# A two-layer graph network: one tile in four of layer 0's sums in fp32, layer 1's clearing and splits made ahead of its gathers, W1 and V2 loaded in four pieces

## The chip, the cores and the metric

One core of one Trainium2 chip runs the whole program. The metric is the device time of one execution in microseconds (us). Engines: TensorE (PE; its weight loads are PEld), VectorE (DVE), ScalarE (ACT), GpSimd (POOL), and SyncE (SP), which here only issues DMAs.

## The reference

1250 nodes with 512 features, 21250 edges sorted by their target `dst`. Layer 0 sums, for each node, messages built from the gathered source row and 64 edge features, and puts the sum through a two-layer MLP; layer 1 does the like with 128 edge features and a GRU update.

```
msg  = relu(x[src] + edge_attr_64 @ W_e + b_e)
h    = (1 + eps) * x + segment_sum(msg, dst)
h    = silu(bn(h @ W1 + b1)); h = silu(bn(h @ W2 + b2)); x = layernorm(x + h)

m    = relu(concat(x[src], edge_attr_128) @ V1.T + b1) @ V2.T + b2
agg  = segment_sum(m, dst)
gi, gh = agg @ W_ih.T + b_ih, x @ W_hh.T + b_hh      # gates r, z, n
out  = layernorm(x + x + bn((1 - z) * n + z * x))
```

All in fp32. Layer 1's `h[src] @ V1h` is computed once for each node into a table, and the edges gather rows of it. V2 is applied after the sum, b2 with the number of edges of each node.

## The kernel before, in words

Every engine runs a list of its own, in the order written, and they meet at semaphores. The edges are cut into 167 tiles of 128 (`TILES`); 4 tiles are a chunk (edge features and one-hot matrices are handled by chunks), 2 tiles a step, 12 tiles a window (`GROUP`), whose targets lie within 128 nodes.

Products of fp32 values are made from fp32r operands, each value split into a high part (the fp32r rounding) and a low part (the rest). For one tile of layer L:

- GpSimd gathers its 128 rows with one indirect DMA (line 429, `gather`) into a ring of 14 slots (`RAW`). The gather of tile t waits until the slot of tile t - 14 is read: for an odd tile `placed`, for an even one `low` (lines 425 to 428).
- SP loads the edge features by chunk into a ring of 3 (`load_chunk`, line 324). ScalarE makes the high part (`high_features`), VectorE the low one (`low_features`, line 1003).
- TensorE multiplies the features with W_e or V1e (`edge_product`, line 527): 2 products a tile in layer 0, 3 in layer 1. For an odd tile ScalarE first copies the gathered row into the bank (`place`, line 827 through `copy`), and the product adds to it; for an even one VectorE adds bank and row (`add_product`, line 1088).
- ScalarE makes `msg_hi`, the relu rounded to fp32r (`message_high`, line 866); VectorE makes `msg_lo`, relu minus `msg_hi` (`low_message`, line 1080). TensorE sums the tile by target: `hot` (one-hot, line 1074 on VectorE) times `msg_hi` and times `msg_lo` (`sum_product`, lines 551 and 552). In layer 1 it also counts the edges (`degrees`, line 565).
- After a window ScalarE copies the sum out of its bank (`sums`), TensorE turns it (`turn_window`, line 574), and VectorE adds it to `agg` at the window's first node (`add_window`, line 1103; the degrees at 1109).

`edges(L)` on each engine is the loop over the steps, with the sum two steps behind the product. Between the two comes layer 0's MLP (line 500, `product`), then the turn back to rows, the first layernorm and the table (`table_dram`), up to about 405 us; behind layer 1's edges come V2, the gates and the output.

What the change touches. In layer 1's gather loop GpSimd, after tile 13's gather, waits and clears `agg[1]` (four memsets, line 471) and `deg_r` (line 472). VectorE, after the last `table_sb`, splits half of the gate weights (`Wh_raw`, lines 1313 to 1315), V1e and v_b2 (to 1323), and then begins `edges(1)`; TensorE waits for V1e's split before `edges(1)` (line 728). SP loads W1 in one DMA behind chunk 9 of layer 0 (line 352), and V2 in one DMA as soon as the table is written (line 379), ahead of chunks 3 and later of layer 1.

## Time and profile before

| | us |
|---|---|
| median of 3 runs | 864.12 (863.08 to 864.97) |
| the profiled execution | 862.61 |
| its span, first to last instruction | 860.8 |
| PE / DVE / ACT / POOL busy | 787.4 / 656.0 / 449.8 / 350.7 |
| gathers of layer 0 start | 3.3 to 222.1 |
| first product of the MLP | 244.7 |
| gathers of layer 1 start | 408.4 to 626.4 |

Times of rows are counted from the span's start. A busy time covers an instruction from its start until its result is out; instructions of one engine overlap, so the distance between two starts can be smaller than the duration of one. In the timeline the brackets at the end of a row say how long the engine was idle before the instruction and what ended that.

### The profile page before, as it was taken

To read this page: it belongs to the slowest core of one execution; us is meant where nothing else is said; L and a number is where in the kernel's file an instruction comes from. 1 tells how busy PE (TensorE), PEld (TensorE's weight loads), DVE (VectorE), ACT (ScalarE), POOL (GpSimd) and SP (SyncE) were. 2 spreads that over 40 slices of the span, in tenths; PEclk is the share of its full clock that TensorE was granted. 3 is DMA by queue.
4 is the path that set the end of the run, shared out by engine and by line. 5 is a ranking of instruction groups with operands and counts; after the bars stand their busy time and mean duration, and the time that the engine had idled before them with its cause. 6 is when DMAs were issued, how large, how long until landed. Compare 5 with 4: busy or idle time off the path is not lost.

```text
span 860.8 us, 11403 instructions
## 1 busy us (share of the span) xinstructions
PE 787.4 (91%) x3714; PEld 623.1 (72%) x3714; DVE 656.0 (76%) x1161; ACT 449.8 (52%) x805; POOL 350.7 (41%) x381
## 2 busy tenths in 40 slices
PE   7888898899879999798879999999999999999993
PEld 5655555555469999686558877887867898989893
DVE  7999999999969924387769999999984363535365
ACT  4888888888744413211457777777761211111122
POOL 6777777777200000021877777777710000000011
PEclk9999999999989999889689999999999999999996
DMA  7999888888500050014868888888830110200011
GB/s 231 339 332 284 253 247 255 249 252 254 202 2 1 1 196 1 1 50 145 254 195 256 256 264 263 256 258 264 250 91 1 73 74 1 74 1 1 1 50 70
DMA packets 49293, 134.38 MB, mean 156 GB/s; under 512 B 8169, under 2 KB 8425, under 8 KB 48848
## 3 DMA queue, kind: packets, MB, share of 16 engines
q0 software_dynamic: 26720, 87.58, 33.9%
q1 hardware_dynamic: 22020, 45.59, 15.7%
q8 instruction: 31, 0.51, 0.2%
q10 hardware_dynamic: 492, 0.45, 0.2%
q14 instruction: 30, 0.25, 0.1%
HBM read 128.47 MB, written 5.12 MB: 155 GB/s over the span
## 4 chain that ended last, share of the span: by engine, by line
PE 51%; DVE 30%; issue 8%; DMA 5%; ACT 2%; POOL 2%; DVEq 0%; ACTq 0%; SPq 0%; POOLq 0%
PE banks L500 37%; DVE msg_lo L1080 10%; DVE raw L1088 7%; PE banks L527 7%; DVE hot L1074 3%; DVE attr_hl L1003 3%; PE banks L551 2%; PE banks L552 2%; DMA raw<-table_dram,src_sb 2%; DMA x_in<-in_x 2%; DMA attr_sb<-in_attr 2%; DVE agg L1103 1%; POOL raw L429 1%; DVE stats L1210 1%; DVE attr_lo L1003 1%
## 5 line engine op out<-in xcount | busy, mean ns | idle before, releaser
L429 POOL DMA_INDIRECT raw<-table_dram,src_sb x167 | 163.1, 976 | 63.7 <-issue 36.1
L429 POOL DMA_INDIRECT raw<-in_x,src_sb x167 | 159.8, 957 | 61.4 <-DVE msg_lo L1080 28.3
L451 POOL TENSOR_TENSOR moments<-moments,minus_half 128x1 f32<-128x1 f32 x32 | 20.3, 635 | 323.5 <-DVE moments L1216 323.5
L551 PE MATMUL banks<-msg_hi,hot 128*128 128x512 f32 x334 | 140.1, 419 | 11.2 <-DVE msg_lo L1080 7.5
L866 ACT ACTIVATE msg_hi<-raw 128x512 fp32r<-128x512 f32 x168 | 105.5, 628 | 66.2 <-DVE raw L1088 64.9
L552 PE MATMUL banks<-msg_lo,hot 128*128 128x512 f32 x334 | 131.6, 394 | 0.0
L1088 DVE TENSOR_TENSOR raw<-banks,raw 128x512 f32<-128x512 f32 x168 | 114.0, 679 | 11.3 <-PE banks L527 8.0
L827 ACT ACTIVATE banks<-raw 128x512 f32<-128x512 f32 x166 | 98.8, 595 | 43.6 <-DMA raw<-table_dram,src_sb 36.4
L1080 DVE SCALAR_TENSOR_TENSOR msg_lo<-raw,msg_hi 128x512 fp32r<-128x512 f32 x168 | 113.5, 676 | 3.3 <-ACT msg_hi L866 3.2
L1080 DVE SCALAR_TENSOR_TENSOR msg_lo<-banks,msg_hi 128x512 fp32r<-128x512 f32 x166 | 112.6, 678 | 2.3 <-ACT msg_hi L866 2.2
L551 PEld LDWEIGHTS banks<-msg_hi,hot 128*128 128x128 f32 x334 | 63.1, 189 | 53.4 <-DVE msg_lo L1080 41.9
L866 ACT ACTIVATE msg_hi<-banks 128x512 fp32r<-128x512 f32 x166 | 96.4, 581 | 0.0
L527 PE MATMUL banks<-We_hi,attr 97*128 97x512 f32 x167 | 74.8, 448 | 10.9 <-ACT banks L827 10.1
L527 PE MATMUL banks<-V1e_hi,attr_hi 128*128 128x512 f32 x167 | 71.4, 428 | 9.2 <-ACT banks L827 7.3
L552 PEld LDWEIGHTS banks<-msg_lo,hot 128*128 128x128 f32 x334 | 63.2, 189 | 9.6
L527 PE MATMUL banks<-V1e_hi,attr_lo 128*128 128x512 f32 x167 | 67.0, 401 | 0.0
L527 PE MATMUL banks<-V1e_lo,attr_hi 128*128 128x512 f32 x167 | 66.9, 401 | 0.0
L527 PE MATMUL banks<-We_lh,attr_hl 128*128 128x512 f32 x167 | 66.2, 397 | 0.0
L527 PEld LDWEIGHTS banks<-We_hi,attr 97*128 97x128 f32 x167 | 31.4, 188 | 39.9 <-ACT banks L827 26.5
L1074 DVE TENSOR_TENSOR hot<-iota_f,in_window 128x512 fp32r<-128x512 f32 x84 | 56.5, 672 | 0.0
L932 ACT ACTIVATE pre<-banks,col 128x512 f32<-128x512 f32 (+2 forms) x36 | 21.4, 604 | 60.5 <-PE banks L500 60.4
L500 PE MATMUL banks<-x_hi,Wg_hi 128*128 128x512 f32 (+2 forms) x144 | 50.7, 352 | 0.6 <-issue 0.6
(167 smaller groups left out, 1645.6 us busy)
## 6 DMA issues: line engine op xcount, KB each, us to landing
attr_sb<-in_attr SPq DMA_DIRECT2D x84, 128.0 KB
attr_sb<-in_attr SPq DMA_DIRECT2D x42, 256.0 KB, 4.0
Wg_raw<-in_Wg SPq DMA_DIRECT2D x3, 1536.0 KB, 6.3
W_raw<-in_W SPq DMA_DIRECT2D x2, 2048.0 KB, 14.4
raw<-in_x,src_sb POOLq DMA_INDIRECT x167, 4.5
raw<-table_dram,src_sb POOLq DMA_INDIRECT x167, 4.1
x_in<-in_x SPq DMA_DIRECT2D x5, 512.0 KB, 11.6
rows<-in_x SPq DMA_DIRECT2D x1, 2560.0 KB, 12.5
```

Source lines behind the costliest of these rows:

```text
L429: pool.indirect_dma_start(rows_of(L, t), None, tables[L], bass.IndirectOffsetOnAxis(ap=src_sb[:, t:t + 1], axis=0)).then_inc(gathered[t % ...
L500: mm = nc.tensor.matmul(acc, a, b, start=start and i == 0, stop=stop and i == len(passes) - 1)
L527: mm = nc.tensor.matmul(edge_bank(t), features, W, start=n == 0 and not odd(t), stop=n == len(passes) - 1, skip_group_check=odd(t))
L551: nc.tensor.matmul(acc, h, msg_hi[L][:, t % MSG, :], start=start, stop=False)
L552: mm = nc.tensor.matmul(acc, h, msg_lo[L][:, t % MSG, :], start=False, stop=stop)
L827: return nc.scalar.activation(to, of, ACT.Copy)
L866: nc.scalar.activation(msg_hi[L][:, t % MSG, :], edge_bank(t) if odd(t) else rows_of(L, t), ACT.Relu).then_inc(relued[L], 1)
L932: nc.scalar.activation(pre[:, c % 2, a:a + w], bank[2 + n % 6][:, 0:w], ACT.Identity, bias=vec("b1", c) if c < KH else vec("b2", c - KH)). ...
L1003: return nc.vector.tensor_tensor(to, value, high.bitcast(F32), ALU.subtract)
L1074: nc.vector.tensor_tensor(hot[L][:, c % HOT, 0:len(tiles), :], nodes, own, ALU.is_equal).then_inc(hot_ready[L], 1)
L1080: nc.vector.scalar_tensor_tensor(msg_lo[L][:, t % MSG, :], edge_bank(t) if odd(t) else rows_of(L, t), 0.0, msg_hi[L][:, t % MSG, :].bitcas ...
L1088: nc.vector.tensor_tensor(rows_of(L, t), edge_bank(t), rows_of(L, t), ALU.add).then_inc(added[L], 1)
```

## The change

Layer 0: of each four tiles the last (t % 4 == 3, function `whole`) gets no low part. ScalarE writes its relu as plain fp32 into `msg_whole`, which lies in the same bytes as `msg_hi[0]`, and TensorE sums it with one fp32 product (hot matrix and message both fp32) instead of two fp32r ones. Waits for `low` count only the tiles that have a low part (`lows`); for whole tiles they go to `relued`.

Layer 1: the clearing of `agg[1]` and `deg_r` stands behind layer 0's last `rstd`, after a wait for the last turn back. V1e and v_b2 are split in layer 0's MLP, behind chunk KH + 1; the Wh split comes after the first one-hots of `edges(1)`. ScalarE waits for the last table product before it begins `edges(1)`. W1 and V2 are loaded in four pieces of 128 rows, each behind one attribute chunk (9 to 12). Several buffers lie at other offsets, and `m_lo` is three tiles in place of one.

```diff
-        agg = [at("agg0", [P, KD, N], F32, B0 + 20 * KB), at("agg1", [P, KD, N], F32, B0 + 20 * KB)]
+        agg = [at("agg0", [P, KD, N], F32, B0 + 20 * KB), at("agg1", [P, KD, N], F32, B0)]
...
+        msg_whole = at("msg_whole", [P, MSG, D], F32, B0 + 68 * KB)
...
+        def whole(L, t):
+            return L == 0 and t % 4 == 3
+        def lows(L, tiles):
+            return len([t for t in range(tiles) if not whole(L, t)])
...
 # SP
-                if c == 3 * RING:
-                    sp.dma_start(W1_raw[:, :, :], W1.rearrange("(k p) n -> p k n", p=P)).then_inc(w1_in, 16)
+                k = c - 3 * RING
+                if 0 <= k < KD:
+                    sp.dma_start(W1_raw[:, k, :], W1[k * P:(k + 1) * P, :]).then_inc(w1_in, 16)
...
-            for i in range(2):
-                sp.wait_ge(table_out[i], 16 * (BLOCKS // 2))
-            sp.dma_start(V2_raw[:, :, :], V2.rearrange("(k p) n -> p k n", p=P)).then_inc(v2_in, 16)
             for c in range(RING, CHUNKS):
                 load_chunk(1, c)
+                if c == 3 * RING:
+                    for i in range(2):
+                        sp.wait_ge(table_out[i], 16 * (BLOCKS // 2))
+                k = c - 3 * RING
+                if 0 <= k < KD:
+                    sp.dma_start(V2_raw[:, k, :], V2[k * P:(k + 1) * P, :]).then_inc(v2_in, 16)
...
 # GpSimd
-                    if L == 1 and t == RAW - 1:
-                        pool.wait_ge(table_mm, BLOCKS)
-                        pool.wait_ge(vb2_split, 1)
-                        (clear agg[1] and deg_r)
...
                 for b in range(BLOCKS):
                     n += 1
                     rstd(n, b % 2)
+                if L == 0:
+                    pool.wait_ge(back_turned, BLOCKS)
+                    (clear agg[1] and deg_r)
...
 # TensorE, sum_product
-                pe.wait_ge(low[L], t + 1)
+                if whole(L, t):
+                    pe.wait_ge(relued[L], t + 1)
+                else:
+                    pe.wait_ge(low[L], lows(L, t + 1))
...
+                if whole(L, t):
+                    mm = nc.tensor.matmul(acc, h.bitcast(F32), msg_whole[:, t % MSG, :], start=start, stop=stop)
+                else:
+                    (the two products of before)
...
 # ScalarE, message_high
+                to = msg_whole if whole(L, t) else msg_hi[L]
...
             def edges(L):
+                if L == 1:
+                    act.wait_ge(table_mm, BLOCKS)
...
 # VectorE, edges
                 one_hots(L, 0)
+                if L == 1:
+                    split_wh()
...
-                        if 0 <= t < TILES:
+                        if 0 <= t < TILES and not whole(L, t):
                             low_message(L, t)
...
 # VectorE, MLP loop, behind if c == KH
+                if c == KH + 1:
+                    (wait for V1h's split; split V1e and v_b2)
...
-            (split Wh, V1e and v_b2)
             edges(1)
```

(Lines in round brackets stand for several lines that moved unchanged.)

## Rows read from the trace of the kernel before

**Rows 1.** The page: share of each engine in the chain that ended last.

```profile
PE 51%; DVE 30%; issue 8%; DMA 5%; ACT 2%; POOL 2%; DVEq 0%; ACTq 0%; SPq 0%; POOLq 0%
```

**Rows 2.** Stretch, us, busy PE, PEld, DVE, ACT, POOL (x count), PEclk, DMA share, GB/s.

```profile
54.00:60.00 6.00, 5.36 (x24) 4.00 (x25) 5.94 (x10) 4.62 (x10) 3.73 (x5) 1.00 1.03 394
84.00:90.00 6.00, 5.64 (x24) 3.58 (x24) 5.91 (x11) 4.71 (x10) 4.42 (x6) 1.00 0.84 264
104.90:120.60 15.70, 14.19 (x54) 8.31 (x53) 15.52 (x25) 13.14 (x26) 11.35 (x12) 1.00 0.85 249
432.00:440.00 8.00, 2.94 (x13) 2.07 (x11) 3.70 (x6) 1.98 (x5) 6.61 (x7) 0.82 0.48 150
440.00:448.00 8.00, 7.93 (x32) 6.32 (x33) 5.09 (x9) 6.02 (x12) 5.88 (x7) 0.75 0.73 214
448.00:456.00 8.00, 8.00 (x42) 6.48 (x41) 8.00 (x15) 6.07 (x12) 6.17 (x7) 1.00 0.84 261
```

**Rows 3.** Timeline of DVE, layer 0: start, duration, what.

```profile
104.89 0.69 DVE L1103 TENSOR_TENSOR agg<-banks,agg 128x512 f32 x1
105.49 0.68 DVE L1088 TENSOR_TENSOR raw<-banks,raw 128x512 f32<-128x512 f32 x1
106.09 0.68 DVE L1080 SCALAR_TENSOR_TENSOR msg_lo<-raw,msg_hi 128x512 fp32r<-128x512 f32 x1
120.60 0.69 DVE L1103 TENSOR_TENSOR agg<-banks,agg 128x512 f32 x1
```

**Rows 4.** Timeline of POOL, layer 0: gathers of tiles 36, 66 and 166.

```profile
50.65 0.94 POOL L429 DMA_INDIRECT raw<-in_x,src_sb  x1 [0.30 <-DVE msg_lo L1080]
91.32 0.94 POOL L429 DMA_INDIRECT raw<-in_x,src_sb  x1 [0.94 <-DVE msg_lo L1080]
222.11 0.94 POOL L429 DMA_INDIRECT raw<-in_x,src_sb  x1 [0.36 <-DVE msg_lo L1080]
```

**Rows 5.** Timeline of DVE, layer 0's last msg_lo.

```profile
237.11 0.68 DVE L1080 SCALAR_TENSOR_TENSOR msg_lo<-raw,msg_hi 128x512 fp32r<-128x512 f32 x1
```

**Rows 6.** Timeline of PE, layer 0: two products and a window's turn.

```profile
105.22 0.40 PE L527 MATMUL banks<-We_hi,attr 97*128 97x512 f32 x1
105.45 0.40 PE L527 MATMUL banks<-We_lh,attr_hl 128*128 128x512 f32 x1
118.50 0.66 PE L574 MATMUL banks<-ident,sums 128*128 128x128 f32 x4 [0.26 <-ACT sums L827]
```

**Rows 7.** Groups by line: an fp32 product of 14 columns, written once in the code.

```profile
L649 PE MATMUL banks<-dst_f,ones 1*128 1x14 f32 x2 | 0.6, 378 | 0.0
```

**Rows 8.** Waits, whole span: engine and line, releaser: us, times, longest.

```profile
DVE stats L1210 <- ACT pre L932: 37.7, 12, 14.5
```

**Rows 9.** Timeline of POOL, layer 1: gathers of tiles 0, 3, 13, 14, 166 and memsets.

```profile
408.38 1.00 POOL L429 DMA_INDIRECT raw<-table_dram,src_sb  x1 [13.26 <-DMA table_dram<-table_sb]
414.54 0.94 POOL L429 DMA_INDIRECT raw<-table_dram,src_sb  x1 [0.30 <-issue]
427.47 0.95 POOL L429 DMA_INDIRECT raw<-table_dram,src_sb  x1 [0.30 <-issue]
428.40 4.42 POOL L471 MEMSET agg<- 128x1250 f32 x4
434.04 0.95 POOL L429 DMA_INDIRECT raw<-table_dram,src_sb  x1 [0.16 <-issue]
626.39 0.94 POOL L429 DMA_INDIRECT raw<-table_dram,src_sb  x1 [0.30 <-issue]
```

**Rows 10.** Timeline of SP, start of layer 1.

```profile
407.68 0.38 SPq L379 DMA_DIRECT2D V_raw<-in_V  x1
```

**Rows 11.** Timeline of DVE, start and end of layer 1's edges.

```profile
405.24 0.95 DVE L1006 CAST Wg_hi<-Wh_raw 128x1536 fp32r<-128x1536 f32 x1
411.53 0.67 DVE L1003 TENSOR_TENSOR attr_lo<-attr_sb,attr_hi 128x512 fp32r<-128x512 f32 x1
636.30 0.67 DVE L1080 SCALAR_TENSOR_TENSOR msg_lo<-raw,msg_hi 128x512 fp32r<-128x512 f32 x1
```

More of the change, by code:

```diff
@@ L465, in _ @@
                     gather(L, t)
-                    if L == 1 and t == RAW - 1:
-                        pool.wait_ge(table_mm, BLOCKS)
-                        pool.wait_ge(vb2_split, 1)
-                        for k in range(KD):
-                            nc.gpsimd.memset(agg[1][:, k, :], 0.0).then_inc(agg_zero, 1)
-                        nc.gpsimd.memset(deg_r[:, :].bitcast(F32), 0.0).then_inc(agg_zero, 1)
                 gather_leftover(L)
@@ L487, in _ @@
                     rstd(n, b % 2)
+                if L == 0:
+                    pool.wait_ge(back_turned, BLOCKS)
+                    for k in range(KD):
+                        nc.gpsimd.memset(agg[1][:, k, :], 0.0).then_inc(agg_zero, 1)
+                    nc.gpsimd.memset(deg_r[:, :].bitcast(F32), 0.0).then_inc(agg_zero, 1)
         @block.tensor
@@ L550, in sum_product @@
                 acc, h = sum_bank[g % 2], hot[L][:, c % HOT, t % CHUNK, :]
-                nc.tensor.matmul(acc, h, msg_hi[L][:, t % MSG, :], start=start, stop=False)
-                mm = nc.tensor.matmul(acc, h, msg_lo[L][:, t % MSG, :], start=False, stop=stop)
+                if whole(L, t):
+                    mm = nc.tensor.matmul(acc, h.bitcast(F32), msg_whole[:, t % MSG, :], start=start, stop=stop)
+                else:
+                    nc.tensor.matmul(acc, h, msg_hi[L][:, t % MSG, :], start=start, stop=False)
+                    mm = nc.tensor.matmul(acc, h, msg_lo[L][:, t % MSG, :], start=False, stop=stop)
                 if L == 1 and t == chunk_tiles(c).stop - 1:
@@ L732, in gate @@
             def gate(m, q, source, g):
-                X_hi, X_lo = ((m_hi, m_lo), (x1_hi, x1_lo))[source]
                 a, w = NODE_CHUNKS[q]
+                X_hi = (m_hi, x1_hi)[source][:, :, a:a + w]
+                X_lo = m_lo[q][:, :, :] if source == 0 else x1_lo[:, :, a:a + w]
                 return [(Wg_hi[m % 2][:, source, k, g, :], Wg_lo[m % 2][:, source, k, g, :],
-                         X_hi[:, k, a:a + w], X_lo[:, k, a:a + w]) for k in range(KD)]
+                         X_hi[:, k, :], X_lo[:, k, :]) for k in range(KD)]
             pe.wait_ge(low[1], TILES)
@@ L853, in place @@
                 elif i >= PLACE_BANKS:
-                    act.wait_ge(low[L], t - 2 * PLACE_BANKS + 1)
+                    last = t - 2 * PLACE_BANKS
+                    if whole(L, last):
+                        act.wait_ge(relued[L], last + 1)
+                    else:
+                        act.wait_ge(low[L], lows(L, last + 1))
                 copy(edge_bank(t), rows_of(L, t)).then_inc(placed[L], 1)
@@ L1130, in split_v2, with split_wh @@
                 split(V2_hi[:, :, ms], V2_lo[:, :, ms], V2_raw[:, :, ms]).then_inc(v2_split, 1)
+            def split_wh():
+                dve.wait_ge(wh_in, 16)
+                wh = [t[:, 1, :, :, :].rearrange("p k g n -> p (k g n)") for t in (Wg_hi[0], Wg_lo[0])]
+                split(*wh, Wh_raw[:, :]).then_inc(wh_split, 1)
             def edges(L):
@@ L1312, in _ @@
                                             ALU.add).then_inc(table_ready, 1)
[L1313 to L1323 removed]
             edges(1)
[L1326 removed]
+            dve.wait_ge(v2_in, 16 * KD)
             for m in range(KD):
```

49 lines of the change are left out of this document (23 added, 26 removed).

## The prediction

> **What bounds the kernel now.** I read the chain of waits by engine and line first [rows 1]: TensorE and VectorE share it, so the bound changes with the stage and no total answers the question. Then the busy time by stretch [rows 2], to see which engine is full where, then the timeline of each engine in the two edge stages (layer 0 from about 15 to 238 us, layer 1 from about 412 to 637 us).
>
> In layer 0 VectorE is the bound. Its instructions start 0.60 us apart with nothing between them [rows 3]. The row of one says 0.68 because it counts the drain, so 0.60 is the price of an instruction removed. A window of 12 tiles takes from one window sum to the next, 120.60 - 104.89 = 15.71 us [rows 3]. GpSimd issues the gathers at a pitch of 1.25 us (0.95 and 0.30 of issue) and waits 0.94 us instead of 0.30 once or so a window for `msg_lo`, from tile 36 on [rows 4]: it is held back by VectorE, but by very little. In layer 1 it is the other way: no gather there waits for longer than 0.30, and the pitch from tile 14 to tile 166 is (626.39 - 434.04) / 152 = 1.2655 us, 15.19 us for 12 tiles [rows 9]. GpSimd is the bound of layer 1, with TensorE and VectorE full beside it (8.00 of 8 us after 448) [rows 2].
>
> **Edit 1, one tile in four summed as fp32 (layer 0).** Tiles 3, 7, ... 163, that is 41 tiles, lose their `msg_lo` on VectorE: 41 x 0.60 = 24.6 us. ScalarE writes as much as before, to another name. A window costs VectorE 15.71 - 3 x 0.60 = 13.91 us. What is late next is the gather issue: 15.19 us for 12 tiles, as in layer 1. So of 1.8 us a window only 0.52 comes at the steady rate, and the rest of the gain is the lag: today VectorE ends 14 tiles behind the gathers, afterwards it follows them.
>
> The end of layer 0's sums is then: gather 36 starts at 50.65, the first to be held at all [rows 4]; 130 more at 1.2655 give 215.2 for the last, now 222.11. The DMA engines are full until about 84 us (share 1.03 at 54 to 60, 0.84 after 84) [rows 2], because x and W1 go in beside the gathers; gathers landing late can hold a slot of the ring of 14. I allow 2 us for it (bounds 0, and 6.9, where the last gather starts no earlier than today). From the last gather to the end of the last `msg_lo` layer 1 takes 636.97 - 626.39 = 10.6 us [rows 9, 11]; layer 0 has one `msg_lo` and the degrees less in that tail and a VectorE with slack, so 9. End: 215.2 + 2 + 9 = 226.2 against 237.7 now [rows 5]. That is **11.5 us** (bounds 5 and 15). What follows (two W1 splits, the last window, the turn to the MLP) is unchanged behind it.
>
> TensorE must bear it. Its products start 0.23 us apart [rows 6]: 12 tiles are 48 x 0.23 + 0.66 for the window's transpositions = 11.7 us. No row shows an fp32 product of 512 columns. A product in fp32 that isn't a transposition appears as two instructions [rows 7]. Four fp32 transpositions, together 512 columns, take 0.66 less the drain of the last, 0.40 - 0.23 = 0.17, thus 0.49 [rows 6]; two instructions at that rate are 0.98. I take 1.0, since these rows stream fp32 at the same clock. Below, it can't beat two of the products of now, 0.46; above, two instructions that each stream 512 columns four times, 8 x 0.23 = 1.84, and two starts of 0.38 uncovered [rows 7], 2.6. At 1.0 a window costs TensorE 11.7 + 3 x (1.0 - 0.46) = 13.3 us, under 15.19; it stays hidden up to 1.62 us a product. ScalarE is busy 13.14 of 15.70 [rows 2] with its work unchanged, hidden too. The place banks are freed earlier, by the activation instead of `msg_lo`.
>
> The Trainium skill (FP8 and Floating Point Precision, "TensorE Precision Notes") says that true fp32 takes four passes through the array; by that the product is 4 x 0.23 = 0.92 us, an estimate, and the sum would not change. No run here shows it yet.
>
> **Edit 2, agg[1] and deg_r cleared before layer 1's gathers.** From gather 13 to gather 14 pass 434.04 - 427.47 = 6.57 us, 1.25 of them the pitch [rows 9]: the clearing costs the gather stream 5.3 us today. It moves behind the last rstd of layer 0, where GpSimd stands idle for 13.26 us before its first gather [rows 9]; 5.6 us of memsets fit. Without that cover they would cost 5.6 again. The other thing that the memset hole does now: TensorE runs dry in it (2.94 of 8 us busy, 13 products against 42) and restarts at a granted clock of 0.75 [rows 2]. Both vanish with it.
>
> **Edit 3, V2 in four pieces behind chunks 9 to 12.** The 1 MB load is issued at 407.68, just before the first gather [rows 10], and the gathers 0 to 3 take 414.54 - 408.38 = 6.16 us instead of 3 x 1.25 [rows 9]: 2.4 us come back. What is put there instead is small, since the attribute chunks 3 and 4 (256 KB each) now go out around 406. SP waits for the table writes at chunk 9 only, long after they have landed.
>
> **Edit 4, splits moved.** V1e and v_b2 go into the second product of layer 0's MLP, where VectorE waits 37.7 us in 12 waits for `pre` [rows 8]; 3.6 us hidden. The Wh split (0.95 and 1.76) stands behind the first attributes; VectorE was through with all of them at 411.5 [rows 11]. From 405.24, where it is free, it now has to wait for a 0.6 us attribute copy and then has two attribute instructions, hot and Wh, 3 x 0.6 and 2.7: done at 410.3, and gather 0, started at 408.38, is not there before 412. Hidden. ScalarE's new wait for the last `table_mm` holds its two attribute copies until just before that 405.24; queued behind them is only the first place, which waits for gather 1 in any case. W1 in four pieces: the attributes queue behind 512 KB instead of 2 MB; nobody waited long for them, worth 0 (bounds -1, and +1 now that VectorE is nearer to them).
>
> A rule speaks against edit 4: the Trainium skill (SBUF — State Buffer, "SBUF: two separate sides") says that a VectorE copy of fp32 within SBUF locks GpSimd out of writing its DMA descriptors. The Wh cast of 0.95 us now comes close to the first gather. By the rule that gather could be up to 0.95 us late, and the sum 18.0 instead of 19.0. In the trace the gather of 408.38 took 1.00 against 0.95 beside a short cast, so it agrees by 0.05 us at most.
>
> Edits 2 and 3 together pull the gather stream of layer 1 forward by 5.3 + 2.4 = 7.7 us. TensorE has 5.06 us idle at 432 to 440 and 10 products of lost clock at 440 to 448 (32 against 42) to give up [rows 2], about 7; with the 2.4 us of earlier start that suffices. I take **7.5 us** (bounds 3 and 8).
>
> **Sum.** 11.5 + 7.5 = 19.0 us. The profiled execution took 862.61 us (span 860.8): 843.6. It lies 1.5 us under the median of 864.12, so the median to expect is 845.1.
>
> **Rivals.**
> A, the DMA engines hold layer 0. A tile costs them 0.85 x 1.31 = 1.11 us, at a pitch of 1.2655 a share of 0.88, so the backlog of x and W1 (4.5 MB) drains more slowly than now, and gathers that land over 10 us late stop the ring. For it: the share above 1 until 84 us. Against: GpSimd was held nowhere before tile 36 in just that stretch. Layer 0 then brings 6 instead of 11.5: 851.
> B, layer 1's other two engines hold. VectorE has 24 instructions, the window sum and the degrees in 12 tiles, 15.2 us, and TensorE is full: neither can make up for a late start at half clock. The hole brings 3 to 4 instead of 7.5: 849. Against: the last lag is that of the tail only.
> C, the other side: fp32 products of 2.2 us (eight streams of 0.23 and one start of 0.38). TensorE's place is between the edge products of a step and the sums; a window is 11.7 + 3 x 1.76 = 17.0 us, 1.27 over today's, times 13.9 windows is 17.7 slower, less 7.5: 874. It makes the whole slower from 1.98 us a product. For it: only that no row shows one; against it: the transpositions' 0.49.
> D, the engines' order in a step (ScalarE's place two tiles ahead, then the message) turns the saved 0.60 into a wait for ScalarE or TensorE, and layer 0 stays at 15.7: 856.
>
> **Chances.** Forecast 0.68, A 0.13, B 0.09, C 0.04, D 0.06. The likeliest one's own range is 840 to 849; A, B and D reach to 856, a layer 0 with neither DMA allowance nor lag to 839. Range 838 to 856. About 0.2% (1.7 us) is what a measurement of this kernel tells from no change. Slower holds C and a mishap of D, 0.05; same 0.02; faster 0.93.
>
> **What would show it.** VectorE's window in layer 0 near 15.2 us instead of 15.71, with waits for the gathered rows or for TensorE in place of none; the last layer-0 gather at about 217 and the first MLP product at 233; the two fp32 instructions together near 1.0 us; gathers 0 to 14 of layer 1 in 17.7 us without a hole; layer 1's last `msg_lo` still 10 to 11 us behind its last gather. Wrong if the fp32 pair is over 1.6 us, if GpSimd still waits for `msg_lo` late in layer 0, or if TensorE still falls to half clock after 424.

## The result, and the profile after

The changed kernel takes **856.59 us** (median of 7, 852.81 to 860.55) against 864.97 for the kernel before beside it (863.08 to 865.76): a ratio of 0.9898, 95% interval 0.987 to 0.9926. The profiled execution took 855.74 us (span 853.9; before 862.61 and 860.8), 6.9 us less. The forecast was 845.1 us, its range 838 to 856. It went the forecast way, with less than half of the forecast gain (8.4 us of 19.0 by the medians). The same kernel on another chip (e12, below) took 853.30 us against 865.16, which is 11.9 us: what the change is worth lies between 8 and 12 us, and one trace each of before and after tells it no finer (before's profiled execution lies 2.4 us under its median, after's 0.9). A ratio can differ from the quotient of the two medians by 0.1%. Two slow executions, 1541.85 us of e14 and 4188.46 us of the kernel before beside e1 to e4, are left out of ratios and of e14's median.

The stages of the two profiled executions, in us, each line read from the timeline of GpSimd, VectorE or TensorE. The fourth, from the first MLP product to layer 1's first gather, is called the dense stage below; a tail is the time from a layer's last gather to the end of its last `msg_lo`.

| | before | after | forecast after |
|---|---|---|---|
| gather of tile 66 | 91.32 | 91.41 | |
| last gather of layer 0 | 222.11 | 221.19 | 217.2 |
| end of layer 0's last `msg_lo` | 237.79 | 234.80 | 226.2 |
| dense stage | 163.69 | 165.37 | 163.7 |
| layer 1, first to last gather | 218.01 | 213.40 | 210.5 |
| layer 1's tail | 10.58 | 10.59 | 10.6 |

The chain of waits of the page after, by engine; it answers to [rows 1]:

```profile
PE 58%; DMA 12%; POOL 11%; DVE 10%; issue 6%; ACT 3%; SPq 0%; DVEq 0%; POOLq 0%; ACTq 0%
```

VectorE fell from 30% to 10%, and in its place stand TensorE (51% to 58%) and GpSimd with the DMAs (together from 7% to 23%). So the change did free the engine that it meant to. The three questions are why the gathers that took over go more slowly than 1.2655 us a tile, why layer 0's tail is 13.61 us behind them, and why the dense stage became longer.

**VectorE's order in layer 0.** Timeline of VectorE after, four window sums, answering to [rows 3]:

```profile
99.21 0.69 DVE L1130 TENSOR_TENSOR agg<-banks,agg 128x512 f32 x1
...
113.17 0.69 DVE L1130 TENSOR_TENSOR agg<-banks,agg 128x512 f32 x1
...
128.28 0.69 DVE L1130 TENSOR_TENSOR agg<-banks,agg 128x512 f32 x1 [0.32 <-PE banks L592]
...
206.81 0.69 DVE L1130 TENSOR_TENSOR agg<-banks,agg 128x512 f32 x1
```

The window up to 113.17 takes 13.96 us: VectorE works off its lag at its own rate, and that is the 13.91 of the forecast. The next takes 15.11, and VectorE now waits for TensorE, which it did not before. The five from 128.28 to 206.81 take 15.71 us each on average. VectorE has caught up with the gathers, and they let a window pass no sooner than VectorE did before (15.71), where 15.2 was forecast. The fp32 product, timeline of TensorE, answering to [rows 6]:

```profile
104.31 1.02 PE L567 MATMUL banks<-msg_whole,hot 128*128 128x512 f32 x2
...
104.77 0.80 PE L539 MATMUL banks<-We_hi,attr 97*128 97x512 f32 x1
...
105.41 0.40 PE L539 MATMUL banks<-We_lh,attr_hl 128*128 128x512 f32 x1
```

From the pair's start to the second product behind it pass 1.10 us; less the 0.23 of the one between, the pair costs 0.87. That is the 1.0 of the forecast, and near the 0.92 that the four passes of the Trainium skill (FP8 and Floating Point Precision, "TensorE Precision Notes") gave.

**GpSimd's gathers.** Groups by line of GpSimd between the gathers of tiles 66 and 166, before: instructions | busy us, mean ns of one | idle us before them, and what ended it:

```profile
L429 POOL DMA_INDIRECT raw<-in_x,src_sb x101 | 95.4, 945 | 37.2 <-DVE msg_lo L1080 21.6 <-issue 10.1 <-ACT banks L827 5.6
```

The same group after:

```profile
L442 POOL DMA_INDIRECT raw<-in_x,src_sb x101 | 100.3, 993 | 30.8 <-issue 25.3 <-ACT banks L846 3.7 <-DVE msg_lo L1107 1.8
```

The idle time fell by 6.4 us, to 101 times the 0.30 that no gather goes below: GpSimd waits for nobody any more. But the gathers themselves became 4.9 us longer, 993 ns each instead of 945. Before, none of them took over 1.00 us; after, 27 do. All 27 begin while VectorE runs an instruction with two inputs in SBUF (20 beside `msg_lo` of an even tile, 7 beside `attr_hl`), 0.07 to 0.50 us behind its start, and end 0.81 to 0.82 us behind its end. Those that begin later under such an instruction take 0.94 to 0.97 us. Before, none of the 101 began beside one. Timeline after, of VectorE and of GpSimd:

```profile
127.28 0.69 DVE L1030 TENSOR_TENSOR attr_hl<-attr_sb,attr_hl 64x512 fp32r<-64x512 f32 x1
127.34 0.58 ACT L890 ACTIVATE msg_whole<-banks 128x512 f32<-128x512 f32 x1
127.36 1.44 POOL L442 DMA_INDIRECT raw<-in_x,src_sb  x1 [0.31 <-DVE msg_lo L1107]
...
221.19 0.95 POOL L442 DMA_INDIRECT raw<-in_x,src_sb  x1 [0.30 <-issue]
```

127.28 + 0.69 + 0.82 is 128.79, and the gather of 127.36 ends at 128.80.

**Layer 0's tail.** Timeline after, of SyncE, ScalarE, TensorE and VectorE:

```profile
209.24 0.39 SPq L366 DMA_DIRECT2D W_raw<-in_W  x1
...
218.20 0.60 ACT L846 ACTIVATE banks<-raw 128x512 f32<-128x512 f32 x1 [4.68 <-DMA raw<-in_x,src_sb]
...
218.85 0.79 PE L539 MATMUL banks<-We_hi,attr 97*128 97x512 f32 x1 [3.78 <-ACT banks L846]
...
234.12 0.68 DVE L1107 SCALAR_TENSOR_TENSOR msg_lo<-raw,msg_hi 128x512 fp32r<-128x512 f32 x1
```

SyncE sends W2's 2 MB right behind the last attribute chunk, at 209.24. Before it went 8 us later, as the chunks came free later (timeline of SyncE before):

```profile
217.32 0.38 SPq L356 DMA_DIRECT2D W_raw<-in_W  x1
```

The gathered rows that are under way together with it are late, and ScalarE, TensorE and VectorE each wait about 4 us. Windows after (columns as in [rows 2]):

```profile
216.00:224.00 8.00, 5.15 (x12) 4.08 (x13) 2.64 (x5) 5.32 (x10) 4.79 (x5) 0.60 1.05 395
...
432.00:440.00 8.00, 8.00 (x43) 6.21 (x42) 7.80 (x15) 6.47 (x13) 6.17 (x7) 1.00 0.81 253
440.00:448.00 8.00, 7.81 (x37) 5.93 (x36) 8.00 (x14) 5.21 (x10) 6.17 (x7) 1.00 0.79 254
448.00:456.00 8.00, 5.91 (x29) 4.56 (x30) 5.13 (x9) 5.33 (x11) 6.17 (x7) 1.00 0.87 291
```

In the first of them the DMA share is 1.05 and the granted clock 0.60, the mean of a stretch partly at 2.4 and partly at 1.2 GHz after TensorE stood (from 219.44 on its products start 0.43 us apart instead of 0.23). Before, VectorE was 14 tiles behind the gathers there, and no engine waited for a gathered row from 205 to 238 us.

**The clearing.** Timeline after, of GpSimd and VectorE at the end of the dense stage:

```profile
390.69 4.39 POOL L498 MEMSET agg<- 128x1250 f32 x4
...
391.12 0.69 DVE L1357 TENSOR_TENSOR table_sb<-banks,vb_bc 128x512 f32<-128x512 f32 x1 [0.19 <-PE banks L512]
...
391.73 4.70 DVE L1320 TENSOR_SCALAR rows<-lnx,moments 98x512 f32<-98x512 f32 x1
...
395.02 1.13 POOL L499 MEMSET deg_r<- 2x1250 f32 x1
```

The hole that the clearing made in layer 1's gathers [rows 9] is gone. But beside GpSimd's clearing VectorE's last normalization takes 4.70 us; the other nine take 0.54. It ends at 396.43, 0.28 us behind the last of GpSimd's five memsets (395.02 + 1.13 = 396.15). The table's last rows, and with them the first gather, come later. The table's addition, which has one input in SBUF and one in PSUM, took its usual 0.69 in the middle of the clearing.

**Layer 1's start.** Timeline after, of VectorE and GpSimd, answering to [rows 9, 11]:

```profile
406.39 1.76 DVE L1030 TENSOR_TENSOR Wg_lo<-Wh_raw,Wg_hi 128x1536 fp32r<-128x1536 f32 x1
...
406.69 2.34 POOL L442 DMA_INDIRECT raw<-table_dram,src_sb  x1 [10.54 <-DMA table_dram<-table_sb]
...
425.60 1.24 POOL L442 DMA_INDIRECT raw<-table_dram,src_sb  x1 [0.30 <-issue]
...
620.09 0.95 POOL L442 DMA_INDIRECT raw<-table_dram,src_sb  x1 [0.30 <-issue]
```

Gathers 0 to 14 take 18.91 us without the hole; 17.7 was forecast, and the first gather's 2.34 is 1.39 over 0.95, which covers the difference. The split of Wh beside it has two inputs in SBUF.

The kernel before had the same thing in the same place. Its gathers 1 and 2 of layer 1 were long too, and each ended 0.82 us behind a VectorE instruction with two SBUF inputs, the second one behind the last of four in a row. Timeline before, of VectorE and GpSimd:

```profile
409.64 0.68 DVE L1003 TENSOR_TENSOR v_b_raw<-v_b_raw,v_b_hi 2x512 f32<-2x512 f32 x1
409.69 1.45 POOL L429 DMA_INDIRECT raw<-table_dram,src_sb  x1 [0.30 <-issue]
...
411.44 2.79 POOL L429 DMA_INDIRECT raw<-table_dram,src_sb  x1 [0.30 <-issue]
...
412.74 0.67 DVE L1074 TENSOR_TENSOR hot<-iota_f,in_window 128x512 fp32r<-128x512 f32 x1
```

Together they are 2.34 us over 0.95, which is the 2.4 us that the prediction put down to V2's load.

### The profile page after: what moved, and what is told of

Read it like the earlier page. It is cut to its first block, busy times and chain, and to the rows that moved or that the text cites. A ratio compares the mean times of both kernels' runs of the same rounds, so it can differ in the third digit from the quotient of the medians.

```text
span 853.9 us, 11369 instructions
## 1 busy us (share of the span) xinstructions
PE 781.4 (92%) x3714; PEld 629.9 (74%) x3714; DVE 638.5 (75%) x1120; ACT 448.8 (53%) x805; POOL 359.6 (42%) x381
## 4 chain that ended last, share of the span: by engine, by line
PE 58%; DMA 12%; POOL 11%; DVE 10%; issue 6%; ACT 3%; SPq 0%; DVEq 0%; POOLq 0%; ACTq 0%
PE banks L512 37%; PE banks L539 10%; POOL raw L442 10%; DMA raw<-in_x,src_sb 7%; PE banks L569 4%; PE banks L570 3%; DMA raw<-table_dram,src_sb 3%; DVE msg_lo L1107 2%; DVE raw L1115 2%; DMA x_in<-in_x 2%; DVE stats L1245 1%; ACT banks L846 1%; PE banks L583 1%; PE banks L592 1%; DVE last L1405 1%
## 5 line engine op out<-in xcount | busy, mean ns | idle before, releaser
L442 POOL DMA_INDIRECT raw<-in_x,src_sb x167 | 168.0, 1006 | 52.3 <-issue 42.3
L569 PE MATMUL banks<-msg_hi,hot 128*128 128x512 f32 x293 | 116.6, 398 | 0.7 <-DVE agg L1130 0.4
L570 PE MATMUL banks<-msg_lo,hot 128*128 128x512 f32 x293 | 115.3, 393 | 0.0
L539 PE MATMUL banks<-We_hi,attr 97*128 97x512 f32 x167 | 87.5, 524 | 20.7 <-ACT banks L846 19.3
L1107 DVE SCALAR_TENSOR_TENSOR msg_lo<-banks,msg_hi 128x512 fp32r<-128x512 f32 x125 | 84.6, 677 | 1.8 <-ACT msg_hi L890 1.6
L890 ACT ACTIVATE msg_hi<-banks 128x512 fp32r<-128x512 f32 x125 | 72.7, 582 | 0.0
L569 PEld LDWEIGHTS banks<-msg_hi,hot 128*128 128x128 f32 x293 | 55.6, 190 | 16.2 <-DVE msg_lo L1107 3.5
L570 PEld LDWEIGHTS banks<-msg_lo,hot 128*128 128x128 f32 x293 | 55.5, 189 | 11.9
```

The costliest lines, as they stand in the source:

```text
L442: pool.indirect_dma_start(rows_of(L, t), None, tables[L], bass.IndirectOffsetOnAxis(ap=src_sb[:, t:t + 1], axis=0)).then_inc(gathered[t % ...
L539: mm = nc.tensor.matmul(edge_bank(t), features, W, start=n == 0 and not odd(t), stop=n == len(passes) - 1, skip_group_check=odd(t))
L569: nc.tensor.matmul(acc, h, msg_hi[L][:, t % MSG, :], start=start, stop=False)
L570: mm = nc.tensor.matmul(acc, h, msg_lo[L][:, t % MSG, :], start=False, stop=stop)
L890: nc.scalar.activation(to[:, t % MSG, :], edge_bank(t) if odd(t) else rows_of(L, t), ACT.Relu).then_inc(relued[L], 1)
L1107: nc.vector.scalar_tensor_tensor(msg_lo[L][:, t % MSG, :], edge_bank(t) if odd(t) else rows_of(L, t), 0.0, msg_hi[L][:, t % MSG, :].bitcas ...
```

## The experiments

**The parts alone.** e1 is the changed kernel without the fp32 tiles:

```
-            return L == 0 and t % 4 == 3
+            return False
```

> The changed kernel without the fp32 tiles: every tile of layer 0 has its low part again; the moved clearing, the splits and the four-piece loads stay. It splits the gain of 8.4 us (864.97 to 856.59) into its two halves. If layer 1's part gives what the trace of after shows there (last gather minus first gather 213.4 us instead of 218.0), this kernel is 4.5 us under the one before, about 860.5. If layer 1's part is worth the 7.5 us that I forecast and the fp32 tiles next to nothing, it is 857.5. W1 in four pieces should show nothing here.

e2 is the kernel before with the fp32 tiles and nothing else of the change (`whole`, `lows`, `msg_whole` and the waits on them).

> The kernel before with the fp32 tiles alone. Theory 1 (the gathers of layer 0 are stretched, and W2's load of 2 MB, sent as soon as the last attribute chunk has gone, now meets the last gathers): layer 0 ends only 3 to 5 us earlier, about 861. The rival, that the fp32 product itself is dear on TensorE, gives the same total but with TensorE full and no waits for gathered rows in layer 0. My forecast for this edit was 11.5 us, 853.5.

Measured: e1 859.36 us, ratio 0.9922 [0.9898, 0.9945]; e2 859.69, 0.9936 [0.9914, 0.9958] (the kernel before took 865.87 on this chip). By the traces each span is 857.4, 3.4 us under before's, and 3.4 + 3.4 is close to the 6.9 of both. By the medians e1 is 6.5 and e2 6.2 us under the kernel before, together 12.7, where the whole measured 8.4 and 11.9: so the two parts bring about as much as each other, and whether they add in full isn't shown. e1 has no long gather between tiles 66 and 166, like the kernel before, and e2 has 26: the fp32 tiles bring them. In e2 the last gather starts at 221.48 as in the changed kernel, and its last `msg_lo` ends at 234.02, 12.54 behind it.

**W2 early (e3).** W2 goes in eight pieces behind attribute chunks 20 to 34 of layer 0:

```
+                if c == 20:
+                    sp.wait_ge(agg_start, BLOCKS)
+                k = (c - 20) // 2
+                if c >= 20 and c % 2 == 0 and k < KH:
+                    sp.dma_start(W2_raw[:, k, :], W2[k * P:(k + 1) * P, :]).then_inc(w2_in, 16)
...
-            sp.wait_ge(agg_start, BLOCKS)
-            sp.dma_start(W2_raw[:, :, :], W2.rearrange("(k p) n -> p k n", p=P)).then_inc(w2_in, 16)
```

(VectorE's wait for W2 counts all eight pieces.)

> The changed kernel with W2 loaded in eight pieces of 256 KB behind the attribute chunks 20, 22, ... 34 of layer 0, instead of in one piece behind the last. If W2's load holds the last gathers (one lands 4 us late at 218, and TensorE falls to half clock behind it), the wait of 4.7 us for a gathered row at the end of layer 0 goes and the kernel gains 4 to 6 us: about 851.5. If the late gather has another cause, the wait stays and the time is that of after, 856.6.

Measured: 851.14 us, 0.9832 [0.9802, 0.9862]. Its last `msg_lo` stands 8.23 us behind the last gather instead of 13.61; the stretch in which TensorE stood is full (windows of e3):

```profile
216.00:224.00 8.00, 7.48 (x31) 4.80 (x30) 6.92 (x12) 6.90 (x14) 6.04 (x7) 1.00 0.74 212
```

The tail that was forecast at 9 us is 8.23 once W2's load is out of it. But the last gather starts at 222.60 here, 1.41 later than in the changed kernel's trace, so layer 0's last `msg_lo` ends 3.97 us sooner (230.83 against 234.80); the medians differ by 5.5 us (against e12's ratio of 0.986 the total is not told apart). e3 sends W2 both sooner and in pieces; which of the two does it isn't separated.

**One DMA per attribute chunk (e4).** Layer 0's chunks come as one DMA of 128 rows, the 64 rows twice in DRAM, in place of two DMAs of 64 rows. The bytes are the same.

```
-                for h in range(P // parts):
-                    sp.dma_start(attr[L][h * parts:(h + 1) * parts, c % RING, :],
-                                 attr_dram[L][:, c * CHUNK * P:(c + 1) * CHUNK * P]
-                                 ).then_inc(attr_in[L][c % RING], 16)
+                sp.dma_start(attr[L][:, c % RING, :], attr_dram[L][:, c * CHUNK * P:(c + 1) * CHUNK * P]
+                             ).then_inc(attr_in[L][c % RING], 16)
```

> The changed kernel with one DMA of 128 rows for each attribute chunk of layer 0 in place of two of 64 rows, the same bytes. If a gather is stretched by SP issuing its DMAs while GpSimd writes the gather's (all 27 gathers over 1.00 us among tiles 66 to 166 stand within 2 us of such an issue), half of the issues halve the excess: 2 to 4 us less, about 853.5. If the stretch comes from the bytes in flight, nothing changes: 856.6.

Measured: 853.32 us, 0.985 [0.9816, 0.9884]. The total was the expected one (though e12, the changed kernel again, came to 853.30 on its chip, so that it shows little), and for another reason than the one written: there are still 23 long gathers between tiles 66 and 166, with a mean of 1002 ns, so SyncE's second issue is not what makes them long. The gain stands before tile 66, which starts at 89.56 instead of 91.41, in the stretch where the DMA engines are full. There the single DMA moves more bytes in the same time. Windows of e12 (the changed kernel again, below):

```profile
22.00:34.00 12.00, 9.28 (x44) 6.52 (x44) 8.09 (x14) 9.56 (x18) 9.26 (x10) 1.00 1.04 323
```

and of e15, with single DMAs, on the same chip:

```profile
22.00:34.00 12.00, 11.68 (x54) 8.33 (x54) 11.04 (x20) 11.57 (x23) 9.26 (x10) 1.00 1.04 389
```

323 against 389 GB/s, of all loads together, at a share of 1.04 in both. Part of that was only put off from the stretch before. Over 10 to 46 us the changed kernel and e4 show:

```profile
10.00:46.00 36.00, 31.32 (x139) 20.98 (x139) 31.36 (x66) 28.72 (x55) 27.77 (x28) 1.00 0.97 298
...
10.00:46.00 36.00, 32.22 (x135) 22.82 (x136) 32.09 (x67) 27.07 (x52) 27.78 (x28) 0.91 0.91 316
```

That is 6% more bytes at a smaller share (0.91 against 0.97). The Trainium skill (SBUF — State Buffer, '"Can I just issue two DMAs to hit both halves?"') says that two DMAs on half of the partitions each don't do the work of one that spans all; these rows agree.

**The clearing later (e7), with W2 early (e8), with single DMAs too (e11), and the port (e10).** e7 puts one wait ahead of the clearing:

```
                     pool.wait_ge(back_turned, BLOCKS)
+                    pool.wait_ge(x1_ready, BLOCKS)
```

> One part is taken away: GpSimd's clearing of layer 1's sums waits until the last block has been normalized, and so no longer runs beside VectorE's last normalization of layer 1's table. Theory (the two instructions exclude each other, VectorE's 4.70 us is its usual 0.54 us and the rest of GpSimd's 4.39 us): the longest of VectorE's normalizations falls from 4.70 to about 0.54 us, the time from the start of the dense stage to layer 1's first gather falls from 165.4 to about 163 us, and the kernel takes about 854 us, 2.5 less than the changed kernel's 856.6. Rival (the 2.7 us come from the other moved work, the splits on ScalarE and VectorE): the long normalization may go, but the first gather starts no earlier, 856.6 us.

> Both repairs together: W2 in eight pieces far ahead of layer 0's last gathers, and the clearing behind the last normalization. If the two causes are independent, their gains add: 851.1 us (W2 early alone) less 2.5, about 848.6 us. Rival (what the dense stage's end gives is eaten by layer 1's first gathers, which then start beside the attribute chunks): 851.1 us.

e10 takes the second SBUF input from VectorE's low parts in layer 0:

```
-    low_part(attr_hl[ED0:P, s, :], attr[0][ED0:P, s, :], attr_hl[ED0:P, s, :])
+    value = attr[0][ED0:P, s, :] if c < 10 else bank[7][ED0:P, :]
+    low_part(attr_hl[ED0:P, s, :], value, attr_hl[ED0:P, s, :])
...
-    ..., edge_bank(t) if odd(t) else rows_of(L, t), 0.0, ...
+    value = edge_bank(t) if odd(t) else rows_of(L, t) if L or t < 40 else bank[7][:, 0:D]
```

> The changed kernel, but from layer 0's chunk 10 and tile 40 on VectorE's low parts of the attributes and of the even tiles' messages take their first input from an unused bank of PSUM instead of SBUF, so that these instructions have one SBUF input instead of two; layer 0's low parts are then not those of the computation. Nothing else changes: same DMAs, same order, same number of instructions. Theory (a gather that starts while VectorE runs an instruction with two SBUF inputs stands until that instruction ends): between tiles 66 and 166 the gathers over 1.00 us fall from 27 to under 6, the last gather starts at 216 to 217 us instead of 221.2, and the kernel takes about 852 us. Rival (they are long because SyncE writes or moves the attribute chunks beside them): still some 25 long gathers, last gather at 221, 856.6 us.

> The two repairs and the attribute chunks of layer 0 in one DMA of 128 rows instead of two of 64. If all three gains add: 851.1 - 2.5 - 3.3, about 845.5 us. Rival (the two DMAs matter only while they are late anyway, and the gain of the single one overlaps with W2's): about 848.5 us, as with the two repairs alone.

Measured: e7 963.01 us, 0.9929 [0.9904, 0.9954]; e8 962.52, 0.994 [0.9909, 0.9972]; e10 967.31, 0.9983 [0.9953, 1.0013]; e11 960.33, 0.9868 [0.9805, 0.993]. These four shared a chip on which the kernel before took 969.85 us, with stretches of 3 to 5 us in both edge stages in which the engines stood together; what caused them stays open, and the totals decide nothing here. The dense stage was left alone by it and can be read: from the first MLP product to layer 1's first gather pass 163.06 us in e7, 162.91 in e8 and 162.29 in e11, against 165.97 in e10, where the clearing stands as in the changed kernel. The traces on the other chips say the same: with the clearing where the change put it the dense stage takes 165.16 to 166.50 us (after, e1, e3, e4, e12, e16), and behind the normalization 162.52 to 162.93 (e14, e15, e17, e18). In e7 the last normalization takes the usual time (timeline of VectorE):

```profile
436.77 0.54 DVE L1321 TENSOR_SCALAR rows<-lnx,moments 98x512 f32<-98x512 f32 x1
```

The rival for e7 falls. And e10 had 11 long gathers between tiles 66 and 166 where e7, e8 and e11 had 29 each.

**The same on another chip, beside the changed kernel itself (e12 to e15).**

> The changed kernel itself once more, as the measure for the three that share its chip. The chip of the four runs before this one took 970 us for the kernel before, with stretches of 3 to 5 us in which all engines stood, so that differences of 2 or 3 us could not be read from their totals. Expected: 27 or so gathers over 1.00 us between tiles 66 and 166, one normalization of about 4.7 us, 165.4 us from the dense stage to layer 1's first gather, 856.6 us.

> As e10 (from chunk 10 and tile 40 of layer 0 VectorE's low parts take their first input from an unused bank of PSUM; layer 0's low parts are then not those of the computation). Theory: 11 long gathers or fewer instead of 27, layer 0's last gather at 217 to 218 us instead of 221.2, and about 853 us. Rival (the long gathers cover a wait that would be there in any case, such as ScalarE's for the gathered rows): the gathers are short, but the last one starts no earlier than 220.5, 856 to 857 us.

> As e8: W2 in eight pieces far ahead of layer 0's last gathers, the clearing behind the last normalization. If the gains add: 5.5 and 2.5 us less than the changed kernel, 848.6 us. Rival (the dense stage's gain is eaten by layer 1's first gathers): 851.1 us.

> As e11: the same two repairs and layer 0's attribute chunks in one DMA of 128 rows. If all gains add: 845.5 us. Rival (the single DMA gives nothing of its own once W2 is early): 848.5 us.

| | median, us (of 4, e14 of 3) | ratio to before (865.16) | last gather | layer 0's tail | dense stage |
|---|---|---|---|---|---|
| e12, the change | 853.30 | 0.986 [0.984, 0.988] | 223.42 | 11.37 | 165.81 |
| e13, one SBUF input | 851.97 | 0.9845 [0.9815, 0.9875] | 221.08 | 12.20 | 164.06 |
| e14, W2 and clearing | 849.04 | 0.9801 [0.9772, 0.983] | 223.71 | 7.97 | 162.92 |
| e15, and single DMAs | 844.78 | 0.9763 [0.9743, 0.9783] | 219.68 | 7.97 | 162.52 |

e13 settles what makes a gather long. Long gathers fell from 30 to 14, and groups by line between tiles 66 and 166 say, for e12:

```profile
L442 POOL DMA_INDIRECT raw<-in_x,src_sb x101 | 101.1, 1001 | 30.8 <-issue 28.9 <-ACT banks L846 1.8
```

and for e13:

```profile
L442 POOL DMA_INDIRECT raw<-in_x,src_sb x101 | 99.1, 981 | 30.8 <-issue 27.8 <-ACT banks L846 2.7 <-DVE msg_lo L1109 0.3
```

All 14 begin beside `hot`, which still has both inputs in SBUF, and none beside the instructions that lost one; in e10 all 11 do. In the changed kernel not one of the 27 began beside `hot`. Timeline of e13, of VectorE and GpSimd:

```profile
132.94 0.68 DVE L1102 TENSOR_TENSOR hot<-iota_f,in_window 128x512 fp32r<-128x512 f32 x1
133.01 1.44 POOL L442 DMA_INDIRECT raw<-in_x,src_sb  x1 [0.30 <-issue]
...
154.73 0.69 DVE L1030 TENSOR_TENSOR attr_hl<-banks,attr_hl 64x512 fp32r<-64x512 f32 x1
154.92 0.95 POOL L442 DMA_INDIRECT raw<-in_x,src_sb  x1 [0.31 <-issue]
```

A gather that starts 0.19 us behind `attr_hl` takes 0.95 with one of its inputs in PSUM; with both in SBUF and started 0.08 us behind it, one took 1.44. Of the 39 gathers that begin in the first 0.5 us of `attr_hl` or a `msg_lo` in e13 none takes over 0.96. Of the numbers expected, 14 long gathers stand for 11, and the last gather came 2.3 us sooner than e12's where 3 to 4 were written; but it came no sooner than in the first trace of the changed kernel (221.08 and 221.19). What the long gathers cost in the total isn't shown: the intervals of e12 and e13 overlap, layer 0's last `msg_lo` ends 1.5 us sooner, and 1.75 us of e13's shorter span stand in the dense stage, where its normalization came through one memset sooner:

```profile
389.95 3.63 DVE L1322 TENSOR_SCALAR rows<-lnx,moments 98x512 f32<-98x512 f32 x1
```

e14 is 0.6% under e12 by the ratios, 4.3 us by the medians (849.04, 848.6 expected), and e15 another 0.4%, 4.3 us (844.78, 845.5 expected; the intervals of e14 and e15 overlap a little). The absolute times came near what was expected because e12 itself ran 3.3 us under the 856.6 that they were counted from: from e12 on, 8.0 and 11.1 us were expected and 4.3 and 8.5 measured (7.0 and 12.1 between the traces). So each repair still gives something behind the other, and that they add in full isn't shown. In e14 GpSimd clears behind the normalization and still has 6.15 us to spare (timeline of GpSimd):

```profile
389.50 4.40 POOL L501 MEMSET agg<- 128x1250 f32 x4 [1.66 <-DVE rows L1323]
...
401.12 2.33 POOL L444 DMA_INDIRECT raw<-table_dram,src_sb  x1 [6.15 <-DMA table_dram<-table_sb]
```

**Which tiles, and Wh (e16 to e18).** e16 sums tiles 2, 6, 10, ... in fp32 instead of 3, 7, 11, ... (`t % 4 == 2`, and the gather into such a tile's slot waits for `relued`).

> The changed kernel with another choice of the tiles summed in fp32: tiles 2, 6, 10, ... instead of 3, 7, 11, .... An odd tile's msg_lo has one input in PSUM, an even tile's has both in SBUF; so VectorE keeps as many instructions per window but every fourth tile has one with two SBUF inputs less (3 instead of 4). Theory: the long gathers between tiles 66 and 166 fall from 27 to 30 to about 20, the last gather starts 1 to 1.5 us sooner, 1 us less than the changed kernel (0.985 instead of 0.986 to 0.990 of the kernel before). Rival (only the number of VectorE's instructions counts): 27 or more long gathers and the changed kernel's time.

e18 is e15 with Wh's split moved up; e17 is e18 with e16's choice of tiles.

```
             def edges(L):
+                if L == 1:
+                    split_wh()
                 for c in range(2):
                     low_features(L, c)
                 one_hots(L, 0)
-                if L == 1:
-                    split_wh()
```

> Every repair together: W2 early, the clearing behind the last normalization, one DMA per attribute chunk, the even tiles summed in fp32, and Wh's split before VectorE's first attribute parts of layer 1 instead of behind its first hot. If all add: 844.8 us (without the last two) less 1 and less 1.4, about 842.5 us, 0.974 of the kernel before. Rival (layer 1's later engines absorb its earlier start): 844.5 us, 0.976.

> The three repairs (W2 early, the clearing later, one DMA per attribute chunk) and Wh's split before the first attribute parts of layer 1. Theory: the first gather of layer 1 then starts beside an instruction of 0.6 us and not of 1.76 us and takes 1.0 to 1.5 us instead of 2.34; about 1 us less than the three repairs alone, 0.975 of the kernel before. Rival (the first gather of a layer is long for another reason, the attribute chunks sent just before it or its own wait for the table): it still takes 2.3 us.

Measured: e16 858.22 us, 0.9908 [0.9889, 0.9927]; e17 846.31, 0.9777 [0.9748, 0.9806]; e18 **843.66**, 0.9742 [0.9726, 0.9758], the fastest of all (before 865.75).

e16 was a miss: 24 long gathers with a mean over the stretch of 1006 ns, no better than the changed kernel's 993 to 1001. But the count moves by itself: e15 and e18, with one and the same layer 0, have 26 and 21 (means 1001 and 983 ns), and e17, with e16's choice of tiles, has 17 (981). So these runs don't tell whether one two-input instruction less helps. Where the gathers fall in VectorE's order must decide it, and this choice may have moved that too (argued, not measured). The end of the layer also came later: from the last `msg_lo` to the MLP 7.38 us instead of 6.52. e17 carries the same 7.38 us and misses its 842.5; with e18 beside it, which differs by the choice of tiles alone, it is 2.65 us longer by the medians and 2.3 by the traces (the intervals overlap a little), 0.86 of it here.

e18 held in the trace. Timeline of VectorE and GpSimd:

```profile
394.56 1.76 DVE L1031 TENSOR_TENSOR Wg_lo<-Wh_raw,Wg_hi 128x1536 fp32r<-128x1536 f32 x1
396.24 1.29 DVE L1031 TENSOR_TENSOR attr_lo<-attr_sb,attr_hi 128x512 fp32r<-128x512 f32 x2
...
396.71 1.09 POOL L442 DMA_INDIRECT raw<-table_dram,src_sb  x1 [6.14 <-DMA table_dram<-table_sb]
```

The first gather takes 1.09 us instead of 2.34, with the same attribute chunks sent ahead of it; so those were not its reason. Gathers 0 to 14 take 18.02 us (18.91 in e15). In the total e18 and e15 are not told apart (0.9742 and 0.9763, the intervals overlap).

## Why the prediction was wrong, by its own steps

The step that failed is edit 1's 11.5 us for layer 0, of which the trace shows 3.0. Its sum took the gathers of layer 0 at layer 1's pitch of 1.2655 us (measured 1.298) with 2 us for the DMA engines, and then a tail of 9 us (measured 13.61). The clearing that edit 2 held to be covered cost 1.7 us in the dense stage, and layer 1 gave 4.6 us of its 7.5.

The shortfall is 12.1 us of the forecast 19.0, in the profiled executions: 8.6 in layer 0, 1.7 in the dense stage, 2.9 in layer 1, less 1.1 that small stretches gave.

- **Edit 1, what VectorE gives up and TensorE pays: right.** The pair costs 0.87 us; rival C is out. VectorE's own window went to 13.96 us, and GpSimd's waits for `msg_lo` between tiles 66 and 166 from 21.6 to 1.8 us. D's numbers came true, a window of 15.7 us later in layer 0 and 856 us in all, but not its mechanism: GpSimd waits for no engine's order, and its own gathers set the window.
- **Edit 1, the last gather at 215.2 + 2: 4.0 us late.** 3.2 us of it come behind tile 66, the rest before. The pitch of 1.2655 was taken from layer 1, as if a gather's length were its own; what it holds over 1.25 was already twelve long gathers, each begun beside a two-input instruction. Between tiles 66 and 166 it was 1.298: 0.30 of issue and 0.993, not 0.945. That the longer gathers there (4.9 us in all) come from VectorE's two-input instructions is shown by the 27 of 27 in the trace and by e10 and e13. Where they hit depends on how the two engines stand to each other; before, GpSimd was often released by VectorE's `msg_lo` (21.6 us of its idle time) and its gathers never began beside such an instruction. That this release is what kept them apart is argued from those rows and not shown; e15 and e18 say that the instructions' number isn't enough, since the same ones hit 26 and 21 gathers.
- **Edit 1, the tail of 9 us: 4.6 late.** The tail without a collision is 8 to 8.2 us (e3, e14, e15), so the term itself was right. In e12 the same 8.6 us of layer 0 fall 6.2 to the last gather and 2.4 to the tail. The prediction asked what GpSimd's earlier gathers collide with only at the start of layer 0 (rival A), and not which load goes out at its end. W2 sits behind the last attribute chunk, that chunk goes when VectorE frees its slot, and so a faster VectorE moved 2 MB from 217.32 to 209.24, in among the last gathers. Sent early it gives back 4.0 us at the end of layer 0 in e3 and 3.1 in e14 (against e12).
- **Rival A, the DMA engines: half right.** Tile 66 came no sooner than before (91.41), where 88.6 and the 2 us allowed gave 90.6. e4 and e15 show that the DMA engines set this stretch: where they move more bytes in the same time, tile 66's gather starts 1.9 us (e4) and 4.3 us (e15 against e14) sooner. All four traces with single DMAs have it at 89.31 to 90.65, all others at 91.32 to 93.78 (the chip of 970 us left out).
- **Edit 2, the clearing: the cover was there, the neighbour was not seen.** GpSimd had the time, and the hole is gone. "GpSimd stands idle" was read as "it costs nothing"; its memsets cost VectorE 4.2 us once, and the dense stage 1.7 (2.9 when undone, in e7 against e10 and e14 against e12). The prediction had the rule at hand and held it only against the cast of Wh.
- **Edit 4, Wh's split at nothing: the sum had the right neighbours and the wrong instruction.** It weighed the cast of 0.95 us; what stood beside the first gather was the subtraction of 1.76, with two inputs in SBUF: 1.39 us on the first gather, of which e18 takes 1.25 back. The reading that was to test the rule, the gather of 408.38 beside a short cast, was wrong too: the cast (407.90 + 0.42) was over, and the gather began 0.03 us behind the start of a subtraction with two SBUF inputs, which did not hold it (why stays open). The two gathers behind it, 1.45 and 2.79 us, were the ones to look at.
- **Edit 3, V2's load: the gain came, for another reason.** Gathers 0 to 3 went from 6.16 to 5.15 us, and to 3.90 in e18. But by the rows of before under Layer 1's start what stretched them was not the load sent at 407.68; it was v_b2's split, the first attribute parts and the first `hot` on VectorE, which now run ahead of them. This is read from their timing, not tried: no run moves V2 alone.
- **What is left of layer 1.** From tile 14 to 166 the gathers take 194.49 us, before 192.35: their excess over 0.95 went from 2.2 to 4.4 us, the same kind of long gather; GpSimd waits for nobody there, so the other two engines of rival B did not hold it. In the other runs with this order of layer 1 the stretch takes 192.57 (e15) to 195.42 us (e14), so this loss differs from one execution to the next. TensorE did not fall to half clock behind 432 (1.00 in the windows above). It stood for 2.10 us before 449.90 behind a gathered row that was late, with a piece of V2 sent at 443.98 and one at 448.72 (that they are the reason is argued from this timing); no gather was held. The 7.5 us became 4.6.
- **The tail of layer 1** stayed at 10.59 us as said.

The Trainium skill (SBUF — State Buffer, "Who interferes with whom") says that VectorE and GpSimd share one pair of SBUF ports, that an instruction of VectorE in a two-port mode excludes GpSimd and is excluded by it for the whole instruction, and that one with two SBUF inputs contends with what of GpSimd reads SBUF. The 4.70 us beside the memsets, the untouched 0.69 of the table's addition and the gathers of e13 all agree. The page infers that `tensor_tensor` leaves a DMA's descriptor writing alone; for these indirect gathers, whose indices lie in SBUF, the 1.44 us beside `attr_hl` and `hot` and the 2.34 us beside Wh's subtraction say otherwise, and the measurement decides.

## What to carry to other kernels

When a faster engine is to free an indirect gather or any other work on GpSimd, list VectorE's instructions beside it by the number of their SBUF inputs, and look in the old trace for gathers that are longer than the others: here it had two, and they were put down to a load. GpSimd's idle time is free only for work that VectorE's neighbours don't exclude. Then follow every buffer that the faster engine frees to the load that waits for it, and ask among which transfers that load now lands: the large one at the end of a stage is the one to send early (here in pieces, with the two not tried apart). A kernel that has slack hides both, so a term that the old trace shows at zero isn't zero once that slack is spent.

## What the runs showed of the hardware

- A gather that begins 0.07 to 0.5 us behind the start of a VectorE instruction with two SBUF inputs ends 0.8 to 0.9 us behind that instruction's end: 1.44 us beside one of 0.69, 2.34 beside one of 1.76, instead of 0.95. With one of the inputs in PSUM: 0.95. One gather behind four such instructions in a row took 2.79 us; one that began 0.03 us behind such an instruction's start took 1.00.
- Five GpSimd memsets in a row, 5.46 us in all, held VectorE's `tensor_scalar` of 0.54 us, begun in the first of them, for 4.70 us, until 0.28 us behind the last; in e13 it came through before the last one, in 3.63. They did not hold a `tensor_tensor` with one SBUF input.
- With the attribute chunks in two DMAs of 64 rows the DMA engines moved 323 GB/s in all from 22 to 34 us, with one DMA of 128 rows 389, at the same busy share (1.04); over 10 to 46 us it is 298 against 316.
- An fp32 product of 512 columns, two instructions, takes 0.87 us from start to start, against 0.46 for the two fp32r products that it replaces.
- One chip took 970 us for the kernel that the others ran in 865 to 866, with the engines standing together for 3 to 5 us at a time.
